# Products of zeros on TensorE after each group of the first and third aggregation of a graph network

## The chip, the core and the metric

The kernel runs on one core of one Trainium2 chip. The metric is the time of one execution in microseconds (us); lower is better. TensorE (PE in the profile) multiplies, VectorE (DVE) and ScalarE (ACT) do elementwise work, GpSimd (POOL) here issues the gathers, SyncE (SP) issues some of the plain DMAs.

## The reference, cut to what matters

Four layers follow each other on 6250 nodes of 256 features; 106,250 directed edges (self loops among them) are sorted by destination. Three times the rows of the source nodes are summed for each destination node.

```python
def _gin_agg(h, src, dst, eps, n_nodes):
    agg = jax.ops.segment_sum(h[src], dst, num_segments=n_nodes)
    return (1.0 + eps) * h + agg

h = _gin_agg(x, src, dst, eps1, n)          # first aggregation, 256 features
h = jax.nn.relu(h @ W1a + b1a)
h = jax.nn.relu(h @ W1b + b1b)
h = _gin_agg(h, src, dst, eps2, n)          # second aggregation, 512 features
h = jax.nn.relu(h @ W2a + b2a)
out = h @ W2b + b2b
...
msgs = h[src] * norm[:, None]               # third aggregation, 256 features
out = jax.ops.segment_sum(msgs, dst, num_segments=N) + b
```

Between the second and third aggregation stands an attention over 64 slices, and behind the third a layer of 8 experts of which each node uses two. Both are untouched by the change.

## The kernel before

**Tiles.** Nodes are split into 49 blocks of 128 (`NB`). The edges of a block are worked off in tiles of 128 edges: POOL gathers the 128 source rows of a tile from a table in HBM into SBUF (line 280, `edge_rows`), DVE makes a matrix of zeros and ones from the edges' destinations (line 295, `onehot`), and TensorE multiplies the two and adds into the PSUM bank of the block, `psA[b % 2]` (line 320; line 330 for those tiles at the end of a block that also hold edges of the next, `early`). The data are fp32, and each such product appears in the trace as two matmul records (passes).

**Groups.** Three tiles make a group (`GT = 3`). Each aggregation has 282 groups and 846 gathers. TensorE waits at the start of a group until its one-hots and gathers are there, and its last product counts up `groups_used`. `edge_rows` is a ring of 8 groups in the first aggregation and of 6 in the other two; POOL waits with the gathers of a group until TensorE has counted the group that had the slot before. DVE waits on the same count for its ring of one-hots.

**What else runs in an aggregation.** Four blocks make a superblock (at the end two of two blocks and one of one: `SUPER`). While the groups of one superblock are summed, the dense work on the one before it is done in 22 steps, put between the groups by `pipeline`. Each engine has its own copy of that order and works it off strictly. `close(b)` takes the sums of a block out of PSUM (DVE, lines 961 and 962, or 1804), transposes them (TensorE, lines 990 or 1907) and copies the transposes (ACT, lines 905 or 1722). The steps of the first aggregation are three dense products on TensorE (lines 1005, 1011, 1017) with ACT and DVE behind each (913, 917, 923, 971). Those of the third are a product (1920), a normalisation and the choice of experts on DVE, transposes (1929, copied by ACT at 1733), gates (1935) and placements (1947, from DVE's tiles of line 1886). The bank `psA` has 512 fp32 columns. The first aggregation uses 257 of them, the second all, the third 256. `zeros` is a constant tile of 128x512 bf16.

Of the kernel before, what the change touches and what calls it, by code (L numbers as in the profile page):

```python
# [35 lines left out]
P = 128  # L36
N = 6250
E = 106250
D = 256
HID = 512  # L40
# [31 lines left out]
SUPER = tuple((b, 4) for b in range(0, 44, 4)) + ((44, 2), (46, 2), (48, 1))  # L72
# [15 lines left out]
def groups_of(b):  # L88

    return groups_before(b + 1) - groups_before(b)  # L90
# [23 lines left out]
def build(nc, a, out):  # L114

    with ExitStack() as whole:
# [59 lines left out]
        def rsqrt(ch, out, x, tmp):  # L176

            v = nc.vector
            ch.link(v.tensor_scalar(tmp.bitcast(I32), x.bitcast(I32), 1, None, ALU.arith_shift_right))
            ch.link(v.tensor_scalar(out.bitcast(I32), tmp.bitcast(I32), -1.0, float(0x5F3759DF), ALU.mult, ALU.add))  # L180
            for _ in range(3):
                ch.link(v.tensor_tensor(tmp, out, out, ALU.mult))
                ch.link(v.tensor_tensor(tmp, tmp, x, ALU.mult))
                ch.link(v.tensor_scalar(tmp, tmp, -0.5, 1.5, ALU.mult, ALU.add))
                ch.link(v.tensor_tensor(out, out, tmp, ALU.mult))

        def pipeline(group, close, piece, begin=None, close_first=False):

# [647 lines left out]
        with ExitStack() as stack:  # L836
            S = Scope(stack, "s1")
            FIRST, SECOND, THIRD = (0, 1, 2, 3), (5, 7, 9, 11), (14, 16, 18, 20)
            edges = Edges(S, table1, T1_W, ((0, D + 1),), FP32, GPB - 1)
            w1a = S.sb("w1a", [P, KD, HID])  # L840
            w1b = S.sb("w1b", [P, KH, HID])
# [135 lines left out]
            def _(pe):  # L977
                mm = nc.tensor.matmul

                def group(b, g):  # L980
                    edges.sums(pe, b, g, psA, s_evac)
                    if b == 0 and g == edges.spare_at:
                        edges.spare_sums(pe, psM[3])

                def close(b):
                    s, q = place_of(b)
# [603 lines left out]
        with ExitStack() as stack:  # L1590
            S = Scope(stack, "s4")

            PRODUCT, NORM, TURNED, GATES = (0, 1, 2, 3), 4, (7, 8, 9, 10), 11
            CHOICE, RANK, PLACED, USED = 12, 16, (17, 18, 19, 20), (18, 19, 20, 21)
            edges = Edges(S, table3, D, ((0, D),), FP32, 1, slots=6)
            w = S.sb("w", [P, KD, D])
            bias = S.sb("bias", [P, D])
# [294 lines left out]
            def _(pe):  # L1892
# [4 lines left out]
                def group(b, g):  # L1897
                    edges.sums(pe, b, g, psA, s_evac)
                    if b == 0 and g == edges.spare_at:
                        edges.spare_sums(pe, psO[1])  # L1900

                def close(b):
                    s, q = place_of(b)
# [315 lines left out]
```

How the kernel before makes its waits and increments, by code:

```python
            def link(self, ins):  # L167
                self.n += 1
                ins.then_inc(self.sem, 1)
                self.eng.wait_ge(self.sem, self.n)
# [94 lines left out]
            def gather(self, pool):  # L265
                for b in range(NB):
                    for i in range(groups_of(b)):
                        g = groups_before(b) + i
                        if g == self.spare_at + 1:
                            with pool.Fori(0, self.spare_count(pool)) as k:
                                pool.wait_ge(self.s_oidx, k * 32 + 32)
                                pool.sem_inc(self.s_ostart, 1)
                                pool.indirect_dma_start(self.o_rows[:, :], None, self.table,
                                                        bass.IndirectOffsetOnAxis(ap=self.o_idx[:, 0:1], axis=0)).then_inc(self.s_orow, 16)
                        if g >= self.SLOTS:
                            pool.wait_ge(self.s_used, g - self.SLOTS + 1)
                        for t in range(tiles_of(b, i)):
                            at = column(b, i) + t
                            pool.indirect_dma_start(
                                self.rows[:, g % self.SLOTS, t, :], None, self.table,
                                bass.IndirectOffsetOnAxis(ap=src_idx[:, at:at + 1], axis=0)
                            ).then_inc(self.s_group[g % self.SLOTS], 16)
# [377 lines left out]
                def first_edges():  # L661
                    dve.wait_ge(s_brow, 16)
                    ch.link(v.tensor_copy(brow_f[:, :], brow[:, :]))
```

## Time and profile before

| | us |
|---|---|
| timed runs, median of 3 | 4537.28 (4523.38 to 4537.72) |
| profiled execution, span from first to last instruction | 4526.2 |
| first aggregation, from its first gather to its last product | 1244.5 |
| second aggregation | 1293.0 |
| third aggregation | 1251.0 |
| gather instructions on POOL, 2538 in all, busy | 2495.4 |
| TensorE matmuls busy in the whole span | 3407.3 |

The three aggregations are 3789 us of the span and are bounded by the time of their groups. "Busy" for TensorE is the union of records whose ends are modelled. The clock that a row shows is the mean of what TensorE was granted, 1.00 being 2.4 GHz and 0.50 being 1.2 GHz.

### The profile page before, as it was taken

To read this page: it belongs to the slowest core of one execution; us is meant where nothing else is said; L and a number is where in the kernel's file an instruction comes from. 1 tells how busy PE (TensorE), PEld (TensorE's weight loads), DVE (VectorE), ACT (ScalarE), POOL (GpSimd) and SP (SyncE) were. 2 spreads that over 40 slices of the span, in tenths; PEclk is the share of its full clock that TensorE was granted. 3 is DMA by queue.
4 is the path that set the end of the run, shared out by engine and by line. 5 is a ranking of instruction groups with operands and counts; after the bars stand their busy time and mean duration, and the time that the engine had idled before them with its cause. 6 is when DMAs were issued, how large, how long until landed. Compare 5 with 4: busy or idle time off the path is not lost. (4 is left out here: it accounts for less than half of the span.)

```text
span 4526.2 us, 40559 instructions
## 1 busy us (share of the span) xinstructions
PE 3407.3 (75%) x12357; PEld 2256.3 (50%) x12359; DVE 1481.5 (33%) x5707; ACT 497.8 (11%) x1161; POOL 2794.2 (62%) x2815
## 2 busy tenths in 40 slices
PE   3577777878878889899999976566556656658997
PEld 2354444545453444444444455345444444438986
DVE  5112121212121433444333445234343343442221
ACT  4010000000110000000000002000000000003432
POOL 4666666666646666666666502666666666635664
PEclk7788888988889999999999987777777778769998
DMA  6333333433349666666666527334334333327887
GB/s 199 90 112 112 111 110 110 131 111 111 109 128 330 194 198 200 193 190 194 195 201 205 170 104 240 108 114 123 115 117 128 115 114 114 119 80 174 203 210 188
DMA packets 321341, 687.10 MB, mean 152 GB/s; under 512 B 58976, under 2 KB 148300, under 8 KB 320854
## 3 DMA queue, kind: packets, MB, share of 16 engines
q0 software_dynamic: 169712, 474.01, 37.9%
q10 hardware_dynamic: 86448, 110.35, 7.4%
q1 hardware_dynamic: 64970, 100.14, 6.8%
q8 instruction: 105, 1.72, 0.2%
q14 instruction: 106, 0.87, 0.1%
HBM read 592.43 MB, written 99.13 MB: 153 GB/s over the span
## 5 line engine op out<-in xcount | busy, mean ns | idle before, releaser
L280 POOL DMA_INDIRECT s_edge_rows<-table,w_src_idx x2538 | 2495.4, 983 | 1235.3 <-issue 712.6
L320 PE MATMUL s_psA<-s_edge_rows,s_onehot 128*128 128x257 f32 (+2 forms) x4932 | 1695.0, 487 | 212.1 <-DMA s_edge_rows<-table,w_src_idx 92.3
L320 PEld LDWEIGHTS s_psA<-s_edge_rows,s_onehot 128*128 128x128 f32 x4932 | 1012.6, 210 | 758.6 <-issue 635.1
L295 DVE TENSOR_SCALAR s_onehot<-w_iota_row,w_dst_l 128x128 f32<-128x128 bf16 x2466 | 531.6, 296 | 28.5 <-PEq L149 16.4
L2031 POOL DMA_INDIRECT acc_rows<-s_y,s_tnode x105 | 166.3, 1584 | 130.7 <-DVE s_y L2154 98.8
L1011 PE MATMUL s_psM<-s_h1T,s_w1b 128*128 128x512 f32 (+2 forms) x448 | 195.2, 582 | 52.5 <-ACT s_h1T L913 49.0
L330 PE MATMUL s_psA<-s_edge_rows,s_early 128*128 128x257 f32 (+2 forms) x648 | 221.3, 468 | 10.2 <-issue 9.0
L1017 PE MATMUL s_psM<-s_w2a,s_hT 128*128 128x512 f32 x392 | 196.3, 647 | 22.7 <-issue 16.6
L2179 PE MATMUL s_psU<-s_xT,s_w 128*128 128x128 f32 x1680 | 208.2, 278 | 0.2 <-ACT s_xT L2085 0.2
L2179 PEld LDWEIGHTS s_psU<-s_xT,s_w 128*128 128x128 f32 x1680 | 199.3, 195 | 0.6 <-issue 0.6
L2189 PE MATMUL s_psD<-moe_w,s_hT 128*128 x840 | 199.5, 381 | 0.0
L971 DVE SCALAR_TENSOR_TENSOR s_own<-s_psM,s_eps,s_b2a 128x512 f32<-128x512 f32 x49 | 36.8, 750 | 451.2 <-ACT s_trow L923 313.3
L961 DVE TENSOR_TENSOR w_degree<-w_degree,s_psA 128x1 f32<-128x1 f32 x49 | 7.4, 152 | 513.7 <-remote 294.4
L1947 PE MATMUL moe_psI<-s_at_tile,s_at_lane 128*128 128x392 f32 x196 | 106.5, 678 | 85.9 <-DVE s_at_tile L1886 72.1
L330 PEld LDWEIGHTS s_psA<-s_edge_rows,s_early 128*128 128x128 f32 x648 | 129.6, 200 | 79.7 <-issue 65.9
L1907 PE MATMUL s_psT<-w_ident,s_agg 128*128 128x128 f32 x98 | 26.3, 362 | 180.7 <-DVE s_agg L1804 117.6
L2189 PEld LDWEIGHTS s_psD<-moe_w,s_hT 128*128 128x128 f32 x840 | 152.4, 191 | 16.6
L1011 PEld LDWEIGHTS s_psM<-s_h1T,s_w1b 128*128 128x128 f32 x448 | 89.5, 208 | 134.1 <-issue 77.1
L2154 DVE SCALAR_TENSOR_TENSOR s_y<-s_psD,s_part,s_yb 128x256 f32<-128x256 f32 x105 | 50.8, 484 | 270.5 <-PE s_psD L2189 257.3
L2094 ACT ACTIVATE s_hT<-s_psU,moe_b 128x128 f32<-128x128 f32 x420 | 119.9, 367 | 169.2 <-issue 101.2
L1017 PEld LDWEIGHTS s_psM<-s_w2a,s_hT 128*128 128x128 f32 x392 | 80.3, 209 | 111.3 <-issue 101.8
L2038 POOL DMA_INDIRECT s_xs<-xl_rows,s_tnode x105 | 103.9, 989 | 38.7 <-issue 31.1
(364 smaller groups left out, 2802.6 us busy)
## 6 DMA issues: line engine op xcount, KB each, us to landing
s_w<-in_L_ffn_W_dram SPq DMA_DIRECT2D x105, 512.0 KB
s_edge_rows<-table,w_src_idx POOLq DMA_INDIRECT x2538
s_swT<-swt_rows SPq DMA_DIRECT2D x12, 1024.0 KB
table<-s_trow ACTq DMA_DIRECT2D x11, 1024.0 KB
own_rows<-s_own ACTq DMA_DIRECT2D x11, 1024.0 KB
s_self_h<-own_rows ACTq DMA_DIRECT2D x11, 1024.0 KB
swt_rows<-s_swT ACTq DMA_DIRECT2D x11, 1024.0 KB
extra_rows<-w_zeros SPq DMA_DIRECT2D x7, 896.0 KB
```

The costliest lines, as they stand in the source:

```text
L280: pool.indirect_dma_start(self.rows[:, g % self.SLOTS, t, :], None, self.table, bass.IndirectOffsetOnAxis(ap=src_idx[:, at:at + 1], axis=0 ...
L295: last = nc.vector.tensor_scalar(into[:, t, :], iota_row[:, q * P:(q + 1) * P], dst_l[:, at + t:at + t + 1], None, ALU.is_equal)
L320: last = nc.tensor.matmul(banks[b % 2][:, 0:w], self.onehot[:, g % self.AHEAD, t, :], self.rows[:, g % self.SLOTS, t, col:col + w], start= ...
L330: last = nc.tensor.matmul(banks[(b + 1) % 2][:, 0:w], self.early[:, b % 2, i * GT + t - (CAP - max(EARLY)), :], self.rows[:, g % self.SLOT ...
L1011: last = mm(psM[m][:, 0:n], w1b[:, c, m * P:(m + 1) * P], h1T[:, c, 0:n], start=c == 0, stop=c == KH - 1)
L1017: last = mm(psM[j][:, :], hT[:, c, j * P:(j + 1) * P], w2a[:, c, :], start=c == 0, stop=c == KH - 1)
L1947: mm(psI[:, 0:SLOT_TILES], at_lane[:, (2 * b + i) % 4, :], at_tile[:, (2 * b + i) % 4, :], start=False, stop=False, skip_group_check=True) ...
L2031: pool.indirect_dma_start(acc_rows, bass.IndirectOffsetOnAxis(ap=tnode[:, t:t + 1], axis=0), y[:, t % 4, :], None, compute_op=ALU.add).the ...
L2038: pool.indirect_dma_start(xs[:, t % RING, :], None, xl3_rows, bass.IndirectOffsetOnAxis(ap=tnode[:, t:t + 1], axis=0)).then_inc(s_xs[t % R ...
L2094: last = ac.activation(hT[:, t % 2, m, :], psU[t % 2][:, m * P:(m + 1) * P], ACT.Relu, bias=b1[:, bass.ds(e, 1), m])
L2179: last = mm(psU[t % 2][:, m * P:(m + 1) * P], w1[:, t % WRING, k, m * P:(m + 1) * P], xT[:, t % 2, k, :], start=k == 0, stop=k == KD - 1)
L2189: last = mm(psD[t % 2][:, 0:D], hT[:, t % 2, k, :], w2[:, bass.ds(e, 1), k, :], start=k == 0, stop=k == KH - 1)
```

## The change

After the products of each group but the last of its block, TensorE also multiplies `zeros` by `zeros`, in bf16, and adds the result into columns of the block's own bank that nobody reads. In the first aggregation these are 8 products of 224 columns (288 to 511), for blocks 0 to 43; in the third, 16 products of 256 columns (256 to 511), for all blocks. They stand behind the instruction that counts up `groups_used`, wait for nothing and count up nothing. In all 209 groups of the first aggregation (1672 products) and 233 of the third (3728 products) have them. Nothing is removed.

```diff
--- before.py
+++ after.py
@@ -183,6 +183,11 @@
                 ch.link(v.tensor_tensor(tmp, tmp, x, ALU.mult))
                 ch.link(v.tensor_scalar(tmp, tmp, -0.5, 1.5, ALU.mult, ALU.add))
                 ch.link(v.tensor_tensor(out, out, tmp, ALU.mult))
+
+        def idle_products(nc, unread, count):
+
+            for _ in range(count):
+                nc.tensor.matmul(unread, zeros[:, 0:P], zeros[:, 0:unread.shape[1]], start=False, stop=False, skip_group_check=True)
 
         def pipeline(group, close, piece, begin=None, close_first=False):
 
@@ -836,6 +841,7 @@
         with ExitStack() as stack:
             S = Scope(stack, "s1")
             FIRST, SECOND, THIRD = (0, 1, 2, 3), (5, 7, 9, 11), (14, 16, 18, 20)
+            IDLE = 8
             edges = Edges(S, table1, T1_W, ((0, D + 1),), FP32, GPB - 1)
             w1a = S.sb("w1a", [P, KD, HID])
             w1b = S.sb("w1b", [P, KH, HID])
@@ -981,6 +987,8 @@
                     edges.sums(pe, b, g, psA, s_evac)
                     if b == 0 and g == edges.spare_at:
                         edges.spare_sums(pe, psM[3])
+                    if b < SUPER[-3][0] and g < groups_of(b) - 1:
+                        idle_products(nc, psA[b % 2][:, D + 32:HID], IDLE)
 
                 def close(b):
                     s, q = place_of(b)
@@ -1592,6 +1600,7 @@
 
             PRODUCT, NORM, TURNED, GATES = (0, 1, 2, 3), 4, (7, 8, 9, 10), 11
             CHOICE, RANK, PLACED, USED = 12, 16, (17, 18, 19, 20), (18, 19, 20, 21)
+            IDLE = 16
             edges = Edges(S, table3, D, ((0, D),), FP32, 1, slots=6)
             w = S.sb("w", [P, KD, D])
             bias = S.sb("bias", [P, D])
@@ -1898,6 +1907,8 @@
                     edges.sums(pe, b, g, psA, s_evac)
                     if b == 0 and g == edges.spare_at:
                         edges.spare_sums(pe, psO[1])
+                    if g < groups_of(b) - 1:
+                        idle_products(nc, psA[b % 2][:, D:HID], IDLE)
 
                 def close(b):
                     s, q = place_of(b)
```

On TensorE, in the first aggregation at the third dense product of blocks 12 to 15, these instructions stand in a row before (in the code after, lines are 5 to 8 higher; 1017 becomes 1025, 990 becomes 998, 320 becomes 325):

```order
L1017 MATMUL s_psM<-s_w2a,s_hT 128x512 x4
L320 MATMUL s_psA<-s_edge_rows,s_onehot 128x257 x6
L990 MATMUL s_psT<-w_ident,s_agg 128x128 x2
L1017 MATMUL s_psM<-s_w2a,s_hT 128x512 x4
L320 MATMUL s_psA<-s_edge_rows,s_onehot 128x257 x6
```

and after the change:

```order
L1025 MATMUL s_psM<-s_w2a,s_hT 128x512 x4
L325 MATMUL s_psA<-s_edge_rows,s_onehot 128x257 x3
L190 MATMUL s_psA<-w_zeros 128x224 x8
L325 MATMUL s_psA<-s_edge_rows,s_onehot 128x257 x3
L190 MATMUL s_psA<-w_zeros 128x224 x8
L998 MATMUL s_psT<-w_ident,s_agg 128x128 x2
L1025 MATMUL s_psM<-s_w2a,s_hT 128x512 x4
L325 MATMUL s_psA<-s_edge_rows,s_onehot 128x257 x3
L190 MATMUL s_psA<-w_zeros 128x224 x8
```

Each group of three is followed by eight products of zeros, so the transposes of line 990 stand 16 products further back.

On TensorE, in the third aggregation at the start of the dense work of a superblock (transposes of the last block's sums, then the products of line 1920), before:

```order
L320 MATMUL s_psA<-s_edge_rows,s_onehot 128x256 x6
L1907 MATMUL s_psT<-w_ident,s_agg 128x128 x2
L320 MATMUL s_psA<-s_edge_rows,s_onehot 128x256 x3
L1920 MATMUL s_psO<-s_w,s_aggT 128x256 x4
L320 MATMUL s_psA<-s_edge_rows,s_onehot 128x256 x3
L1920 MATMUL s_psO<-s_w,s_aggT 128x256 x2
```

and after (1907 becomes 1918, 1920 becomes 1931):

```order
L190 MATMUL s_psA<-w_zeros 128x256 x16
L1918 MATMUL s_psT<-w_ident,s_agg 128x128 x2
L325 MATMUL s_psA<-s_edge_rows,s_onehot 128x256 x3
L190 MATMUL s_psA<-w_zeros 128x256 x16
L1931 MATMUL s_psO<-s_w,s_aggT 128x256 x4
L325 MATMUL s_psA<-s_edge_rows,s_onehot 128x256 x3
L190 MATMUL s_psA<-w_zeros 128x256 x16
L1931 MATMUL s_psO<-s_w,s_aggT 128x256 x2
```

Sixteen products of zeros now stand between every group and the dense product behind it.

## Rows read from the trace of the kernel before

**Rows 1.** First line of the page.
```profile
span 4526.2 us, 40559 instructions
```

**Rows 2.** Busy time in the three aggregations: stretch, length, busy by engine (instructions), clock, DMA.
```profile
71.50:1316.00 1244.50, 936.52 (x2966) 591.34 (x2966) 243.51 (x1078) 126.64 (x213) 816.12 (x847) 0.86 0.39 112
1333.00:2626.00 1293.00, 1155.03 (x3278) 599.08 (x3278) 509.92 (x1573) 97.44 (x155) 858.47 (x848) 0.95 0.68 204
2783.00:4034.00 1251.00, 749.26 (x2674) 566.60 (x2674) 482.07 (x2149) 38.79 (x109) 823.78 (x847) 0.76 0.41 120
```

**Rows 3.** The gathers in the first aggregation and what ended POOL's idle time before them.
```profile
L280 POOL DMA_INDIRECT s_edge_rows<-table,w_src_idx x737: 951/957/1072, 179.3 to 1239.5; - x185
...
  remote: 106.7, 37
  PE s_psA L320: 31.9, 20
  PE s_psA L330: 3.9, 3
```

**Rows 4.** The gathers in the second aggregation and what ended POOL's idle time before them.
```profile
L280 POOL DMA_INDIRECT s_edge_rows<-table,w_src_idx x833: 951/957/2895, 1349.9 to 2599.2; - x167
...
  DMA s_edge_rows<-table,w_src_idx: 92.2, 32
  PE s_psA L320: 65.6, 44
  PE s_psA L330: 16.6, 6
```

**Rows 5.** The gathers in the third aggregation and what ended POOL's idle time before them.
```profile
L280 POOL DMA_INDIRECT s_edge_rows<-table,w_src_idx x801: 951/957/1993, 2800.1 to 3959.3; - x161
...
  DMA s_spare_dst<-dst_pad: 121.1, 49
  PE s_psA L320: 23.5, 20
  PE s_psA L330: 11.1, 4
```

**Rows 6.** TensorE by line, first aggregation: busy us, mean ns | idle before, releasers.
```profile
L1011 PE MATMUL s_psM<-s_h1T,s_w1b 128*128 128x512 f32 x352 | 173.6, 636 | 44.0 <-ACT s_h1T L913 40.5 <-issue 3.2
...
L990 PE MATMUL s_psT<-w_ident,s_agg 128*128 128x128 f32 x84 | 20.5, 333 | 100.2 <-DVE s_agg L962 71.2 <-issue 29.0
```

**Rows 7.** Timeline of the first aggregation: start, us, engine, line [idle before <-releaser].
```profile
562.00 3.59 PE L1017 MATMUL s_psM<-s_w2a,s_hT 128*128 128x512 f32 x8
...
565.44 2.77 PE L320 MATMUL s_psA<-s_edge_rows,s_onehot 128*128 128x257 f32 x12
...
579.07 0.60 ACT L923 ACTIVATE s_trow<-s_psM 128x512 f32<-128x512 f32 x1 [20.12 <-DMA x_xl<-in_x_dram]
...
580.90 0.69 PE L990 MATMUL s_psT<-w_ident,s_agg 128*128 128x128 f32 x2 [12.70 <-DVE s_agg L962]
```

**Rows 8.** Two short windows.
```profile
572.00:576.00 4.00, 0.00 (x0) 0.00 (x0) 0.00 (x0) 0.00 (x0) 2.86 (x3) 0.50 0.37 99
2778.00:2786.00 8.00, 0.00 (x0) 0.10 (x1) 3.55 (x18) 0.00 (x0) 3.20 (x6) 0.50 0.56 158
```

**Rows 9.** TensorE by line, third aggregation.
```profile
L1947 PE MATMUL moe_psI<-s_at_tile,s_at_lane 128*128 128x392 f32 x176 | 95.1, 673 | 71.7 <-DVE s_at_tile L1886 57.9 <-DMA x_xl<-in_x_dram 8.3 <-issue 5.4
...
L1907 PE MATMUL s_psT<-w_ident,s_agg 128*128 128x128 f32 x90 | 24.6, 367 | 180.7 <-DVE s_agg L1804 117.6 <-issue 63.1
L1929 PE MATMUL s_psT<-w_ident,s_xl 128*128 128x128 f32 x88 | 22.0, 341 | 64.2 <-ACT s_xl3T L1733 40.9 <-issue 23.2
```

**Rows 10.** Timeline of the third aggregation.
```profile
3099.50 0.38 PE L1907 MATMUL s_psT<-w_ident,s_agg 128*128 128x128 f32 x2
...
3111.19 0.38 ACT L1722 ACTIVATE s_aggT<-s_psT 128x256 f32<-128x256 f32 x1 [25.50 <-DMA s_swT<-swt_rows]
```

**Rows 11.** The one load of zeros as weights that the trace of before has.
```profile
L1895 PEld LDWEIGHTS moe_psI<-w_zeros x1: 105/105/105, 2782.2 to 2782.2; 128*128 128x128 bf16 x1
```

## Prediction

> **What bounds the kernel now.** I first took the span, 4526.2 us [rows 1]; the median of the timed runs, 4537.28, lies 11.1 above it, and I make the sum in the span's time and add it to the median. Then the windows of the three aggregations [rows 2]. They hold 1244.5 + 1293.0 + 1251.0 = 3788.5 us, 84% of the span. The reader is to see that their lengths hardly differ though TensorE is busy for 936.5, 1155.0 and 749.3 us of them, that is 75%, 89% and 60%. So TensorE's amount of work is not what sets the pace. What the three share is 846 gathers each. A gather takes 957 ns at the median [rows 3 to 5], and the three stretches spend 816, 858 and 824 us in them [rows 2].
>
> Next, what POOL waits for [rows 3 to 5]. Some 0.3 us between one gather and the next are plain issue. Beyond that POOL waits at the start of a group for `groups_used`, which only TensorE counts up. The profile puts part of that wait down to TensorE's products (lines 320 and 330), and part to "remote" or to a DMA that has nothing to do with it; in that part the products were finished by the trace long before. By gather:
>
> first: 106.7/737 = 0.145 us not explained, 35.8/737 = 0.049 explained, 0.193 together;
> second: 92.2/833 = 0.111 and 82.2/833 = 0.099, together 0.209;
> third: 121.1/801 = 0.151 and 34.6/801 = 0.043, together 0.194.
>
> The timeline shows what the unexplained part looks like [rows 7]. Line 1017 has its records from 562.00 to 565.6 and the next two groups follow until 568.2. ACT's copy of that product starts at 579.07, 13.5 us after the end of the records, and TensorE stands until 580.90 for DVE, which was queued behind that copy. In the third aggregation transposes end at 3099.9 and the copy of them starts at 3111.19 [rows 10]. ACT was idle in both cases. The other engines learn of TensorE's work late, by 10 us and more, and the trace doesn't say why. In such a gap the granted clock falls: from 572 to 576 it is 0.50, 1.2 GHz, with TensorE idle [rows 8]. Over an aggregation it is 0.86, 0.95 and 0.76 [rows 2], lowest where TensorE does least.
>
> **The change part by part.** Nothing is removed; 1672 products of 224 columns and 3728 of 256 are added. The trace has no full record of a bf16 product. Its cost from both sides: eight passes of 512 columns in fp32 start 565.44 - 562.00 = 3.44 us apart [rows 7], 0.43 us each or two cycles of 2.4 GHz per column. A bf16 product may go at the same two cycles: 0.187 and 0.213 us. Or at one: the only load of bf16 weights takes 105 ns for 128 columns [rows 11] while the clock is 0.50 [rows 8], 126 cycles of 1.2 GHz. I take one cycle per column, since that row has the same tile of zeros and the same type: 0.093 and 0.107 us at the full clock, twice that at half. The load of the weights lies under the product before it, as the fp32 passes at exactly two cycles per column show. Sum at the full clock: 1672 x 0.093 = 155 us in the first aggregation, 3728 x 0.107 = 399 us in the third. With two cycles it would be 313 and 794 us.
>
> The Trainium skill ("TensorE: Matmul & The Clock Gate", Back-to-back issue gap) gives N / 2.4 + 2.5 ns between bf16 products at the full clock. By that formula they would be 96 and 109 ns, 161 and 406 us together; no run here shows it yet.
>
> How much of this lies beside other work: by the busy times of today's clock, 936.5 + 155 = 1092 of 1244.5 us and 749.3 + 399 = 1148 of 1251.0, 88% and 92% [rows 2]. At the second aggregation's clock the old parts would be nearer 936.5 x 0.86/0.95 = 848 and 749.3 x 0.76/0.95 = 599, an upper bound of what a warmer clock gives, and the shares 81% and 80%. The second aggregation lives with 89%. So in both the products fit into time in which TensorE now waits, and the cover is POOL's gathers. What stands behind a product of zeros in TensorE's queue is the next group or the next dense step. Each may start up to 8 x 0.093 = 0.75 us or 16 x 0.107 = 1.7 us later, and with it the counts for which POOL, ACT and DVE wait. The rings of eight and six groups absorb such a delay as long as TensorE catches up.
>
> The price or gain is then read in POOL's wait per gather. If a denser TensorE brings the unexplained part to the second aggregation's 0.111, that returns (0.145 - 0.111) x 846 = 29 us and (0.151 - 0.111) x 846 = 34 us. Against it the explained part rises. From 0.049 at a share of 75% to 0.099 at 89%, a straight line gives 0.070 at 80 to 81%: +0.021 x 846 = 18 us in the first and +0.027 x 846 = 23 us in the third. Net: -63 + 41 = -22 us, and the forecast 4537 - 22 = 4515 us. Ends of this case: no return of clock and the full 0.099 in both (+89 - 63 = +26), and no rise at all (-63).
>
> **The rivals.**
>
> *A. TensorE keeps its waits and becomes the bound of the third aggregation (slower).* In the window of the third, TensorE waits 57.9 + 117.6 + 40.9 = 216 us for ACT and DVE at the placements and the two transposes [rows 9]. If those waits stay as long as they are and the products come on top, the stretch takes 1148 + 216 = 1364 us instead of 1251: +113, total 4650. The first aggregation has 40.5 + 71.2 = 112 us of such waits [rows 6] and would need 1092 + 112 = 1204, below its 1244.5. It decides from where more than 103 of today's 216 us remain behind the products. For it: gaps like that of 12.7 us [rows 7] are far longer than the 0.75 or 1.7 us of zeros ahead of them, and behind a gap each group of the third now costs 1.7 us more to catch up. Against it: the second aggregation has few such gaps at 89%. At two cycles per column this rival would add some 500 us, which I give almost nothing.
>
> *B. A warm clock removes the late counts (much faster).* If the late counts come from a TensorE that stands and cools, products behind each group would bring them on time. All of POOL's waits are 0.193 x 846 + 0.194 x 846 = 327 us; half of it gone gives 4537 - 164 = 4373. For it: the lower the clock, the larger the unexplained part per gather (0.111 at 0.95, 0.145 at 0.86, 0.151 at 0.76). Against it: total waits per gather are the same 0.19 to 0.21 in all three, so what a dense TensorE saved in one part it lost in the other. The Trainium skill (same page, Loop structure matters more than you think) says that a TensorE that waits between bursts does the next burst at the lower clock; the trace agrees with the 0.50 in the gap, and on that rule the change should help. It says nothing of counts that come late.
>
> *C. Nothing happens.* POOL's gathers and their issue set the pace, the long gaps stay long, and the zeros run in time that nobody needs: 4537. For it: the equal totals of 0.19 to 0.21. The change would then not do what products into unread columns can only be for, to hold the clock.
>
> **How the numbers follow.** Forecast 0.43 (4515, its own range 4474 to 4563), A 0.27 (4550 to 4650), B 0.16 (4373 to 4470), C 0.14 (4523 to 4551). A measurement of this kernel can tell about 0.3%, 14 us. Faster by more than that: 0.30 of the forecast and all of B, 0.46. Within it: 0.09 of the forecast, 0.13 of C, 0.22. Slower: 0.04, A, and 0.01 of C, 0.32. The range of 4400 to 4640 leaves out the far half of B and the end of A, less than 2 in 10.
>
> **What would show it.** Right: mean clock of the first and third aggregation at 0.9 or above; records of line 190 spaced by 0.09 to 0.11 us; POOL's unexplained wait near 0.11 us per gather; TensorE's gaps over 4 us fewer, not only shorter; the second aggregation unchanged. A shows as POOL's wait put down to line 325 rising above 0.1 us per gather in the third aggregation, which grows alone. B shows as ACT's copies starting within a microsecond of the product they wait for. C shows as a clock that stays at 0.86 and 0.76. The prediction is wrong if a product costs two cycles per column, if the counts come late for a reason that more TensorE instructions make worse, or if catching up behind a gap with 16 products in every group empties POOL's ring.

## The result, and the profile after

The changed kernel takes 4599.24 us (median of 4 runs, 4589.41 to 4612.92) beside 4531.9 us for the kernel before: a ratio of 1.0156, 95% interval 1.0136 to 1.0176. It is slower by 1.56% (the two medians lie 67 us apart). A later run of the same kernel gave 1.0169 (1.0146 to 1.0193), and the kernel before against itself 0.9992 (0.9976 to 1.0008). The forecast was 4515 us with a small gain; the time lies in the range given, on the wrong side of no change.

First the head of the page. The span has grown by 78.3 us against [rows 1]; the row PEclk gives the granted clock of TensorE in 40 slices of the span.

```profile
span 4604.5 us, 51359 instructions
...
PE 3892.9 (85%) x17757; PEld 2691.5 (58%) x17759; DVE 1477.1 (32%) x5707; ACT 498.0 (11%) x1161; POOL 2796.1 (61%) x2815
...
PEclk6799989999999999999999987899998989879998
```

Then the same windows of the three aggregations as in [rows 2]: stretch, length, busy us and instructions of PE, PEld, DVE, ACT and POOL, clock, DMA.

```profile
72.00:1341.00 1269.00, 1085.70 (x4638) 726.33 (x4638) 244.80 (x1080) 127.08 (x213) 815.27 (x847) 0.91 0.39 110
1358.60:2647.20 1288.60, 1150.83 (x3278) 596.26 (x3278) 506.70 (x1570) 97.12 (x155) 860.71 (x847) 0.95 0.68 204
2804.40:4111.60 1307.20, 1089.69 (x6402) 871.06 (x6402) 478.43 (x2149) 38.85 (x109) 823.17 (x847) 0.90 0.39 115
```

The reader is to see three things. The clock went where the change sends it: from 0.86 to 0.91 and from 0.76 to 0.90, while the second aggregation stays at 0.95. The second aggregation is as long as it was (1288.6 after 1293.0). And the first is 24.5 us longer, the third 56.2 us. The rest of the kernel adds some 2 us, so the loss lies in the two stages that have the products. In the third TensorE's busy time grew by 1089.7 - 749.3 = 340.4 us and the rest of its time shrank from 501.7 to 217.5 us, by 284.2: it gave back most of what the products took, and the difference is the 56.2 us.

Next come the gathers, with what ended POOL's idle time before them, in the first aggregation and in the third; these answer to [rows 3] and [rows 5].

```profile
L285 POOL DMA_INDIRECT s_edge_rows<-table,w_src_idx x735: 951/957/1081, 180.2 to 1259.8; - x184
...
  remote: 112.8, 48
  PE s_psA L325: 47.9, 26
  PE s_psA L335: 11.2, 5
```

```profile
L285 POOL DMA_INDIRECT s_edge_rows<-table,w_src_idx x810: 951/957/1820, 2819.7 to 4039.1; - x162
...
  DMA s_spare_dst<-dst_pad: 133.2, 71
  PE s_psA L325: 62.0, 44
  PE s_psA L335: 26.3, 16
```

The values by gather, in the prediction's terms: the unexplained wait was 0.145 us in the first aggregation and is 112.8/735 = 0.153; it was 0.151 in the third and is 133.2/810 = 0.164. It should have fallen to 0.111. The explained wait rose from 0.049 to 59.1/735 = 0.080 and from 0.043 to 88.3/810 = 0.109.

The products themselves cost what they were priced at. This is the timeline of the third aggregation: start, us, engine, line.

```profile
3197.00 1.91 PE L190 MATMUL s_psA<-w_zeros 128*128 128x256 bf16 x16
3198.75 0.38 PE L1918 MATMUL s_psT<-w_ident,s_agg 128*128 128x128 f32 x2
```

Sixteen products of 256 columns take 3198.75 - 3197.00 = 1.75 us, 0.109 us each; those of 224 columns start 0.096 us apart, by the median. By the formula of the Trainium skill ("TensorE: Matmul & The Clock Gate", Back-to-back issue gap) it is 109 and 96 ns, and the trace agrees. The sum in the two stages is 1672 x 0.096 + 3728 x 0.109 = 567 us at the full clock.

What TensorE waits for has changed its nature. By line in the third aggregation (busy us, mean ns | idle us before it, releasers), beside [rows 9]:

```profile
L190 PE MATMUL s_psA<-w_zeros 128*128 128x256 bf16 x3728 | 489.4, 282 | 73.2 <-issue 61.9 <-DVE s_spare_own L1796 10.4
...
L1958 PE MATMUL moe_psI<-s_at_tile,s_at_lane 128*128 128x392 f32 x185 | 83.4, 582 | 12.6 <-DVE s_at_tile L1895 11.5 <-issue 1.1
...
L1918 PE MATMUL s_psT<-w_ident,s_agg 128*128 128x128 f32 x96 | 23.4, 326 | 51.1 <-issue 37.0 <-DVE s_agg L1813 14.1
```

The waits for DVE before the placements went from 57.9 to 11.5 us and before the transposes from 117.6 to 14.1. In their place stand 61.9 us before products of zeros that are put down to "issue": TensorE stands and waits for nothing that the profile shows. These products have nothing to wait for, and all 3728 are in the records, so no missing record makes the gap. What is left is that TensorE does not have its next instruction yet; that is an inference, since the trace shows no such event.

### The profile page after: what moved, and what is told of

Its sections match the earlier page's. It is cut to its first block and busy times, and to the rows that moved or that the text cites. A ratio compares the mean times of both kernels' runs of the same rounds, so it can differ in the third digit from the quotient of the medians.

```text
span 4604.5 us, 51359 instructions
## 1 busy us (share of the span) xinstructions
PE 3892.9 (85%) x17757; PEld 2691.5 (58%) x17759; DVE 1477.1 (32%) x5707; ACT 498.0 (11%) x1161; POOL 2796.1 (61%) x2815
## 5 line engine op out<-in xcount | busy, mean ns | idle before, releaser
L325 PE MATMUL s_psA<-s_edge_rows,s_onehot 128*128 128x257 f32 (+2 forms) x4932 | 1644.8, 471 | 129.3 <-issue 74.1
L325 PEld LDWEIGHTS s_psA<-s_edge_rows,s_onehot 128*128 128x128 f32 x4932 | 954.3, 200 | 638.6 <-issue 545.2
L190 PE MATMUL s_psA<-w_zeros 128*128 128x256 bf16 (+1 forms) x5400 | 698.6, 277 | 97.9 <-issue 86.3
L190 PEld LDWEIGHTS s_psA<-w_zeros 128*128 128x128 bf16 x5400 | 540.0, 101 | 249.3 <-issue 138.7
L1019 PE MATMUL s_psM<-s_h1T,s_w1b 128*128 128x512 f32 (+2 forms) x448 | 182.1, 548 | 12.0 <-ACT s_h1T L919 8.6
L1025 PE MATMUL s_psM<-s_w2a,s_hT 128*128 128x512 f32 x392 | 185.3, 618 | 1.0 <-ACT s_hT L923 1.0
L1013 PE MATMUL s_psM<-s_aggT,s_w1a 128*128 128x512 f32 (+2 forms) x224 | 111.7, 644 | 65.0 <-issue 52.7
L1731 ACT ACTIVATE s_aggT<-s_psT 128x256 f32<-128x256 f32 x49 | 18.8, 383 | 1043.6 <-DMA s_swT<-swt_rows 483.5
L1019 PEld LDWEIGHTS s_psM<-s_h1T,s_w1b 128*128 128x128 f32 x448 | 79.9, 192 | 81.8 <-issue 70.5
```

Of the source, the lines that this page charges most:

```text
L190: nc.tensor.matmul(unread, zeros[:, 0:P], zeros[:, 0:unread.shape[1]], start=False, stop=False, skip_group_check=True)
L325: last = nc.tensor.matmul(banks[b % 2][:, 0:w], self.onehot[:, g % self.AHEAD, t, :], self.rows[:, g % self.SLOTS, t, col:col + w], start= ...
L1013: last = mm(psM[m][:, 0:n], w1a[:, c, m * P:(m + 1) * P], aggT[:, c, 0:n], start=c == 0, stop=c == KD - 1)
L1019: last = mm(psM[m][:, 0:n], w1b[:, c, m * P:(m + 1) * P], h1T[:, c, 0:n], start=c == 0, stop=c == KH - 1)
L1025: last = mm(psM[j][:, :], hT[:, c, j * P:(j + 1) * P], w2a[:, c, :], start=c == 0, stop=c == KH - 1)
```

## Experiments

All ratios are against the kernel before on the same chip in the same hour. Stage lengths are from the first gather of a stage to the end of its last product of gathered rows in the trace: 1244.5, 1292.3 and 1251.2 us before, 1268.8, 1288.6 and 1307.2 in the change.

My first theory was rival A in a new form: time of TensorE is what counts, and 567 us of products are more than its waits give back. Its rival: not the time of the products but their number.

**Products in the third aggregation only.**

```diff
-            IDLE = 8
+            IDLE = 0
```

> No products of zeros in the first aggregation, 16 of 256 columns per group in the third as in the change. The third aggregation grew by 56 us and the first by 24 us in the profiles. Time theory (TensorE's own time per group came too near to POOL's 3.8 us per group, so it cannot catch up behind a gap and POOL's ring stays full): the two stages are independent, so this gives about 56/80 of the loss, ratio 1.010 to 1.014, with the first aggregation back at 1245 us. Instruction theory (the number of instructions in TensorE's queue costs): two thirds of the products are here, ratio also near 1.010. If the loss came from the two together or from elsewhere (instruction fetches over the whole run), the first aggregation would stay long.

Measured: 1.0096 (1.0076 to 1.0115). The third aggregation takes 1303.5 us, the first 1248.9. **The first only** (the third's 16 set to 0):

> 8 products per group in the first aggregation, none in the third. If the two places add up: 1.0156 less 1.0096 of the third alone, 1.006 (1.004 to 1.008), with the first aggregation 24 us longer than before and the third unchanged. Rival, that the first's loss is noise of its start: 1.001 or less.

Measured: 1.0042 (1.0026 to 1.0057), the first aggregation 1261.2 us and the third 1248.1. The two places add up to 1.0138, within the interval of the change. The first aggregation's loss is real though small.

**A quarter, half, and fewer products that take longer.** In order: 2 and 4 products in place of 8 and 16; the same 2 and 4 with fp32 zeros; 4 and 8.

> A quarter of the products: 2 per group in the first aggregation, 4 in the third. They take 0.19 and 0.44 us per group at the full clock instead of 0.76 and 1.74. Time theory: TensorE keeps its room to catch up, POOL's explained wait stays near that of before (0.05 us per gather) and the ratio is 0.993 to 1.002; with a clock that rises a little. Instruction theory: a quarter of the loss, ratio near 1.004. If the loss is linear in the added time, also 1.004.

```diff
-                nc.tensor.matmul(unread, zeros[:, 0:P], zeros[:, 0:unread.shape[1]], ...)
+                nc.tensor.matmul(unread, zeros[:, :].bitcast(FP32)[:, 0:P], zeros[:, :].bitcast(FP32)[:, 0:unread.shape[1]], ...)
```

> A quarter of the products, but of zeros read as fp32, which take four cycles per column instead of one (two passes of two cycles): the same added time per group as the change (0.75 and 1.7 us), with half of its matmul and weight-load records. Time theory: the same loss as the change, ratio 1.012 to 1.019. Instruction theory: half of the loss or less, ratio 1.002 to 1.008.

> 4 products per group in the first aggregation and 8 in the third, half of the change. If only the number of instructions counts, this stands where 2 and 4 fp32 products stood, which are two instructions pairs each: 1.008 (1.006 to 1.010), although its columns take half as long. If the column time counts, it lies below that: 1.003 to 1.006. Straight line between none and the change: 1.008; between a quarter (1.0009) and the whole: 1.006.

**Sixteen as before, but of 8 columns.**

```diff
-                nc.tensor.matmul(unread, zeros[:, 0:P], zeros[:, 0:unread.shape[1]], ...)
+                nc.tensor.matmul(unread[:, 0:8], zeros[:, 0:P], zeros[:, 0:8], ...)
```

> As many products as in the change (8 and 16 per group) but of 8 columns: nearly no column time, yet the same number of products and loads of weights. A product then costs what its load of weights costs, some 0.05 us at the full clock by the rows of line 190 (128 columns at one cycle), so 0.4 and 0.9 us per group, half of the change. Time theory: a third of the loss or less, ratio 0.998 to 1.006. Instruction theory: all of the loss, ratio 1.012 to 1.019.

Measured, with the number of multiplications recorded for the zeros and their array time by the median spacing in each trace. An fp32 product is recorded as two passes and is also two in the stream of instructions: the instruction queue moves 126 packets in the fp32 kernel with its 1350 calls, as many as in the half with its 2700.

| kernel | multiplications | array time, us | ratio (95%) | clock |
|---|---|---|---|---|
| quarter | 1350 | 142 | 1.0009 (0.9995 to 1.0022) | 0.882 |
| half | 2700 | 283 | 1.0066 (1.0046 to 1.0086) | 0.895 |
| fp32, a quarter of the calls | 2700 | 561 | 1.0080 (1.0058 to 1.0103) | 0.925 |
| 8 columns | 5400 | 135 | 1.0135 (1.0111 to 1.0159) | 0.878 |
| the change | 5400 | 567 | 1.0156 (1.0136 to 1.0176) | 0.916 |

The table decides between the two theories. Rows with the same number lie close together, with intervals that overlap, though their array time differs by a factor of two or four; rows with nearly the same array time (142 and 135, 561 and 567) lie far apart. The products of 8 columns start 0.025 us apart, so in the third aggregation they add about 93 us of array time where the change adds 406, and the stage still takes 1289.9 us in place of 1307.2: 38.7 of the 56 us are there without the columns. (The Trainium skill, TensorE: Matmul & The Clock Gate, Wait — 56ns, not 53.3ns?, says that starts of products never come closer than about 25 ns however small they are; the trace agrees.) What counts is mostly how many instructions TensorE is given. The loss isn't linear from zero: the first 1350 cost next to nothing, the next 1350 26 us, as ratios times 4535.

What the short ones do can be seen in a timeline of that kernel, with TensorE's rows only:

```profile
3311.60 0.69 PE L325 MATMUL s_psA<-s_edge_rows,s_onehot 128*128 128x256 f32 x2 [0.26 <-issue]
3312.14 0.19 PE L190 MATMUL s_psA<-w_zeros 128*128 128x8 bf16 x2
3313.03 0.26 PE L190 MATMUL s_psA<-w_zeros 128*128 128x8 bf16 x4 [0.70 <-issue]
3314.45 0.17 PE L190 MATMUL s_psA<-w_zeros 128*128 128x8 bf16 x1 [1.16 <-issue]
3315.17 0.18 PE L190 MATMUL s_psA<-w_zeros 128*128 128x8 bf16 x1 [0.56 <-issue]
3316.58 0.17 PE L190 MATMUL s_psA<-w_zeros 128*128 128x8 bf16 x1 [1.23 <-issue]
3317.32 0.33 PE L190 MATMUL s_psA<-w_zeros 128*128 128x8 bf16 x7 [0.57 <-issue]
```

From 3312.14 on the zeros, which wait for nothing, come in ones, twos and fours, at 0.7 us or twice 0.7 us from each other; then seven at once. In the third aggregation of this kernel about 100 products start 0.66 to 0.76 us after the product before on the same line; in the change there are about 35, in the kernel before about a dozen. Over the stretch from 2820 to 4040 TensorE's idle time put down to "issue" is 19% of the 8-column kernel and 10.5% of the change. Before, it was 14.6% from 2800 to 3960, but half of that at the transposes (lines 1907 and 1929).

**The same number of instructions without the array.**

```diff
-            for _ in range(count):
-                nc.tensor.matmul(unread, zeros[:, 0:P], zeros[:, 0:unread.shape[1]], ...)
+            for i in range(2 * count):
+                nc.tensor.sem_inc(W.idle[i % 4], 1)
...
+        W.idle = [W.sem(f"idle{j}") for j in range(4)]
```

> Each product of zeros is replaced by two increments of a count that nobody reads, given by TensorE's queue: as many instructions as a product's weight load and multiplication (10,800 in all), but none for the array. Theory 'the number of TensorE instructions, whatever they do': as the short products, 1.013 (1.010 to 1.016). Theory 'the array: each small load and multiplication costs TensorE or what it reads': nothing is left, 1.000 (0.998 to 1.002). Both theories expect the granted clock of before, 0.86. If the stretches in which TensorE's instructions come one by one at steps of about 0.7 us come from the supply of instructions, they grow here too.

Measured: 1.073 (1.0697 to 1.0764), far outside both. The timeline of the third aggregation says why:

```profile
3295.82 1.03 PE L326 MATMUL s_psA<-s_edge_rows,s_onehot 128*128 128x256 f32 x4
3300.99 0.66 PE L1919 MATMUL s_psT<-w_ident,s_agg 128*128 128x128 f32 x2 [4.15 <-issue]
...
3304.06 2.41 PE L326 MATMUL s_psA<-s_edge_rows,s_onehot 128*128 128x256 f32 x6
3309.93 2.30 PE L1959 MATMUL moe_psI<-s_at_tile,s_at_lane 128*128 128x392 f32 x3 [3.46 <-issue]
```

Behind a group come 32 increments, and TensorE's next row is 4.15 us after the end of the last: up to 0.13 us per increment on TensorE's queue, more than a whole product. The third aggregation takes 1553.7 us. So this run doesn't hold the cost of an instruction equal, and can't decide what I made it for. It shows one thing in passing. In the first aggregation, with 16 increments per group and no product added, the stage takes 1266.9 us, as with the change's products (1268.8). So a loss of that size needs nothing in the array. It doesn't follow that the change's loss has the same cause, since 16 increments at up to 0.13 us hold TensorE's queue longer than 8 products at 0.096 us do.

**Is the ring too short?** If TensorE frees slots late now and then, deeper rings should help. Two slots more in the third aggregation, with the change and without it:

```diff
-            edges = Edges(S, table3, D, ((0, D),), FP32, 1, slots=6)
+            edges = Edges(S, table3, D, ((0, D),), FP32, 1, slots=8)
```

> The change, with eight instead of six slots of three tiles in the third aggregation's ring of gathered rows. If the loss there is that TensorE frees slots too late for the gathers, two slots more (8 us of gathers) take most of it away: third aggregation 30 us or more shorter than in the change, ratio 1.003 to 1.009. If the gathers are slowed otherwise (the DMA queues' own limit, or what they share), the third stays 55 us longer and the ratio 1.013 to 1.017.

> The kernel before, with eight instead of six slots in the third aggregation's ring. Theory 'before, the gathers wait there for slots whose release comes late now and then, while TensorE has time to catch up': two slots more take half of the third's 145 us of waits away, ratio 0.985 (0.980 to 0.992). Theory 'TensorE sets the pace there too': as in the change with eight slots, nothing, 1.000.

Measured: 1.0168 (1.0148 to 1.0187) and 1.0018 (1.0008 to 1.0027), the third aggregation 1306.8 and 1258.9 us. My theory of bursts fell, twice. The kernel before, with eight slots:

```profile
L280 POOL DMA_INDIRECT s_edge_rows<-table,w_src_idx x801: 951/957/1997, 2799.2 to 3959.7; - x161
...
  DMA s_spare_dst<-dst_pad: 117.1, 44
  PE s_psA L320: 24.7, 16
  PE s_psA L330: 16.4, 5
```

The unexplained wait is 117.1 us where [rows 5] have 121.1. What changed is only how far the gathers run ahead. From the end of a group's last gather to the start of its products, by the median of the stage's 282 groups, passed 10.7 us before and 18.3 with eight slots (18.5 and 27.2 with the zeros). The ring fills up, however long it is. That is what is seen when the consumer sets the pace. In both kernels, then, TensorE's side (its work, the late counts, its waits for what others do with its results) sets the pace of the third aggregation, and its idle time wasn't spare. Which of these three it is, this test doesn't say.

**Less work for TensorE.** The one-pass products cut the rows to bf16, and nothing else is left out:

```diff
+            def half(self, x):
+                return x.bitcast(BF16).rearrange("p (c two) -> p c two", two=2)[:, :, 1] ...
...
-                        last = nc.tensor.matmul(..., self.onehot[:, g % self.AHEAD, t, :],
-                                                self.rows[:, g % self.SLOTS, t, col:col + w], ...
+                        last = nc.tensor.matmul(..., self.half(self.onehot[:, g % self.AHEAD, t, :]),
+                                                self.half(self.rows[:, g % self.SLOTS, t, col:col + w]), ...
```

> The change, but in the third aggregation the products of gathered rows read only the upper halves of their fp32 numbers, as bf16 (so the rows are cut short before they are added; nothing else is left out). Each group's products become one pass where fp32 takes two: 930 products fewer in the records, and about 1.07 us less of array time per group, 300 us in the stage. Theory 'with the zeros TensorE sets the third aggregation's pace, with its work and the time in which it has no instruction': the stage falls back to 1,251 us or below, ratio 1.000 to 1.004, although all zeros are still there. Theory 'the zeros slow the gathers in another way (a shared path, late counts)': it stays at 1.013 or above.

> The kernel before with the same shorter products of gathered rows in the third aggregation. Theory 'before, TensorE does not set the pace there': 0.995 to 1.002. Theory 'what TensorE does always sets it, by late releases in proportion to its work': clearly faster, 0.985 or less, and then the next run but one says how much of it comes back in the change.

Measured: 1.0138 (1.0116 to 1.016) with the zeros, 0.9954 (0.9938 to 0.997) without. The third aggregation takes 1274.4 and 1235.0 us. So 300 us of array time at the full clock (930 products, two passes of 0.216 us against one of 0.114) gives 33 and 16 us back. By the records TensorE's busy time in the stage fell by 204 and 282 us, though its clock fell too, to 0.80 and 0.58: without the zeros most of the shorter products start 0.213 us apart, which is the lower clock. TensorE's array time isn't the bound either. The window of the first of the two:

```profile
2820.00:4040.00 1220.00, 855.25 (x5273) 611.95 (x5272) 452.53 (x1979) 37.60 (x103) 803.11 (x825) 0.80 0.40 119
```

TensorE is busy for 855 of 1220 us there, its clock is 0.80, and 283 us of its idle time are "issue": by the waits, 303 times. In the change the same stretch has 139 such times. TensorE does a group faster, and then has no instruction.

**The same zeros in longer rows**, 32 behind every second group:

> The change, with the third aggregation's zeros in every second place, 32 at a time in place of 16 at each: the same number within one in a hundred. If TensorE's total counts (work and missing instructions, averaged over the ring): 1.0156 as the change (1.013 to 1.018). If a long row of short instructions runs TensorE out of them, more idle time without a cause in the trace and over 1.02.

Measured: 1.0184 (1.0155 to 1.0214), the third aggregation 1313.0 us. The interval overlaps that of the change. The idle time under "issue" is somewhat larger (163 us where the change has 128). How the zeros are grouped makes no difference to the time that is clear of the noise.

**More time at the ends of blocks.** With the next theory (the waits for TensorE's own late counts at a block's end set the pace) I moved these ends:

```diff
-                    if g == 1 and b and not close_first:
+                    if g == 3 and b and not close_first:
...
-                        if s and i == 2 + k * (len(turns) - 2) // STEPS:
+                        if s and i == 5 + k * (len(turns) - 5) // STEPS:
```

> The kernel before, with each block's transposes on TensorE and ScalarE two groups later (behind the fourth group of the next block, where they stood behind its second) and all the steps of a super-block three groups later. Theory 'TensorE's waits at a block's end for its own late counts set the pace': of the 180 us of waits before the transposes in the third aggregation and the 100 in the first, half or more go, ratio 0.97 to 0.985. Theory 'the gathers set the pace with late releases that no order on TensorE changes': 1.000 (0.997 to 1.003).

> The same later ends of blocks, with the products of zeros of the change. Under the first theory the zeros have used up those waits already, and this gives little: 1.010 to 1.015. Under the second theory also as the change, 1.013 to 1.017; so this run only says whether the zeros' loss stays when the order has more room.

> The kernel before with both the one-pass products of the gathered rows (cut to bf16) and eight slots in the third aggregation. With less work TensorE waited 173 us for gathered rows there while the gathers still waited 123 us for slots: bursts. Theory 'TensorE stands still for longer than the ring lasts, then catches up': two slots more take half of the gathers' waits away, ratio 0.984 (0.980 to 0.990). Theory 'ring depth never matters, the counts come late whatever the lead': 0.995 as without the slots.

> The kernel before, with only the steps of a super-block two groups later and the blocks' ends where they stood. The wait of the dense products for the copies of the transposes (10.6 us at its longest) goes, the wait for the blocks' sums stays: by the first theory a small gain, 0.993 to 1.000; by the second 1.000.

Measured: 1.0135 (1.0118 to 1.0152), 1.0194 (1.0177 to 1.0211), 1.0003 (0.9994 to 1.0013) and 1.0067 (1.005 to 1.0084). But these four can't be read by the expectations, since the kernel before itself took 4084.66 us in this set (13 runs, 4078.36 to 4092.16), on the chip on which it had taken 4529.23 in the set before. It has no trace in this condition; the four kernels made from it do. The windows of the later ends without zeros, then with them:

```profile
62.50:1144.00 1081.50, 889.43 (x2904) 568.15 (x2905) 242.53 (x1074) 123.17 (x203) 816.07 (x847) 0.93 0.45 129
1184.70:2352.80 1168.10, 1109.91 (x3253) 577.64 (x3254) 498.21 (x1541) 93.57 (x152) 865.18 (x847) 0.98 0.74 225
2532.90:3631.90 1099.00, 722.81 (x2653) 539.47 (x2654) 466.49 (x2087) 37.23 (x106) 832.66 (x847) 0.85 0.46 136
```

```profile
62.90:1143.60 1080.70, 997.44 (x4575) 695.75 (x4576) 243.64 (x1075) 123.08 (x203) 815.68 (x847) 0.98 0.46 129
1183.90:2351.40 1167.50, 1112.58 (x3252) 579.50 (x3253) 498.35 (x1542) 93.50 (x152) 867.05 (x847) 0.98 0.74 225
2531.60:3649.50 1117.90, 1003.48 (x6380) 827.79 (x6381) 468.01 (x2088) 38.05 (x106) 831.90 (x847) 0.98 0.46 134
```

And the gathers of the first aggregation in the kernel with the zeros:

```profile
L285 POOL DMA_INDIRECT s_edge_rows<-table,w_src_idx x846: 952/957/1080, 62.7 to 1135.3; - x170
...
  issue: 249.8, 820
...
  PE s_psA L325: 7.0, 23
  PE s_psA L335: 0.6, 2
```

Here the unexplained waits are gone, from every kernel of the set: no "remote" stands among the releasers, and 7.6 us are left of the 172 us of waits in the change's first aggregation. The gathers alone make up the aggregations, 1081 us for 846 of them. TensorE's "issue" time is nearly gone too, and the starts at a distance of 0.7 us with it (none in the zeros of the second kernel). In this condition the first aggregation holds 1672 products of zeros for nothing: 1081.5 and 1080.7 us. The third is 18.9 us longer, 1117.9 after 1099.0, with TensorE busy for 1003 us of it. The two kernels stand to each other as 1.0194/1.0135 = 1.0058. The later ends themselves cost 57 us there. They can win nothing where the gathers bind, and they put the last steps of each stage off: outside the three aggregations lie 799.5 us of the span with them, and 735 in the kernel whose ends stand where they stood, with lighter products and eight slots. That kernel takes 4084.6 us: less work for TensorE and a deeper ring give nothing here.

So I ran the change and the kernel before once more, unaltered.

> The change, unaltered. Where the kernel before takes 4,085 us in this job: if the loss is made by late counts and missing TensorE instructions, it falls to what two kernels with and without the zeros differed by there (1.0194 against 1.0135), 1.006 (1.002 to 1.009), and the gathers wait for slots as rarely as without the zeros. If the loss is TensorE's added work whatever the condition, 1.0156 again. Where the kernel before takes 4,530 us again: 1.0156 (1.013 to 1.018), a repetition.

> The kernel before, unaltered, for its trace: a ratio of 1.000 (0.998 to 1.002) in either case. Where it takes 4,085 us: gathers that wait for slots once or twice per aggregation, TensorE waiting for gathered rows for a fifth of the time, and no row of instructions at 0.7 us.

Measured: 1.0169 (1.0146 to 1.0193) and 0.9992 (0.9976 to 1.0008); the kernel before took 4529.53 us, so the condition was back and this is a repetition. The stages agree with the first traces: 1271.7, 1288.7 and 1306.9 us for the change, 1247.8, 1287.7 and 1248.2 for the kernel before. The change alone without the late counts wasn't measured; the pair with later ends is the nearest.

**How late the counts come, in every trace.** Two distances can be read in all traces: for each of POOL's waits of over 1 us, from the recorded end of the product that frees the slot to the gather (median); and for the 49 copies of the transposes on ACT (lines 1722 and 905 of the kernel before), how many start over 2 us after the transposes ended and ACT was free. First and third aggregation:

| kernel | POOL's waits over 1 us | from product to gather, us | late copies of 49 |
|---|---|---|---|
| before, two traces | 51, 60; 59, 57 | 11.8, 11.1; 11.5, 11.6 | 17, 18; 16, 21 |
| quarter | 55, 64 | 7.1, 7.6 | 3, 18 |
| half | 66, 81 | 7.8, 6.5 | 20, 31 |
| fp32, a quarter of the calls | 72, 91 | 7.3, 4.9 | 24, 22 |
| 8 columns | 79, 107 | 6.8, 5.0 | 27, 30 |
| increments | 71, 118 | 7.8, 0.3 | 22, 0 |
| the change, two traces | 82, 113; 84, 116 | 4.9, 3.5; 5.0, 3.5 | 25, 20; 28, 23 |
| the four of the 4085 us set | 0, 0 to 4 | none, 0.3 | 0, 0 |

In the set at 4085 us every copy follows its transposes at once:

```profile
2805.89 0.38 PE L1907 MATMUL s_psT<-w_ident,s_agg 128*128 128x128 f32 x2
2806.31 0.38 ACT L1722 ACTIVATE s_aggT<-s_psT 128x256 f32<-128x256 f32 x1 [19.84 <-PE s_psT L1907]
```

So the late counts are in all traces of the other sets and in none of this one. The zeros don't make POOL's counts later: the more TensorE is given, the sooner they come behind their product, and the more waits there are. Why both go together isn't shown. The quarter's first aggregation has almost no late copies and is as long as before (1248.5 us), and with the increments the third has none and is the longest (1553.7): late copies and a long stage can be had one without the other.

No kernel here that computes the whole reference beats the kernel before.

## Why the prediction was wrong

**Right:** the price of a product (0.093 and 0.107 us forecast, 0.096 and 0.109 measured), the clock of both aggregations at 0.9 or above, fewer long gaps (TensorE's gaps over 4 us in the third went from 39 with 364 us to 17 with 107), and an unchanged second aggregation.

**The step that failed first** is "if a denser TensorE brings the unexplained part to the second aggregation's 0.111". It had 63 us of gain in it, and went to 0.153 and 0.164: in the stretches' terms +7 and +11 us. The inference was from three stages in a row, clock against unexplained wait, and the second aggregation differs from the others in more than its clock. With this term at zero the forecast would have been 41 us slower than before.

**The second** is the straight line that gave the explained part +18 and +23 us. It measured (0.080 - 0.049) x 846 = 26 us in the first and (0.109 - 0.043) x 846 = 56 us in the third. It drew the wait over TensorE's busy share, and a share can't tell 16 instructions of 0.11 us from one of 1.7. The second aggregation's 89% is reached with 3278 multiplications, the third's 83% in the change with 6402. By the table above, the number weighs more than the time. The share put into the line was too low as well: 80 to 81% forecast, 1085.7/1269.0 = 86% and 83% measured, since the old work didn't shrink with the clock as much as its upper bound allowed. With the measured shares the same line gives +31 and +30 us. So in the first aggregation the line nearly holds (26), and in the third (56) it fails. The two steps together give +100 us of waits; the stages grew by 24.5 + 56.2 = 81, since a gather behind a wait no longer pays the whole of its 0.3 us of issue: all of POOL's time between gathers, issue included, grew by 26 and 50 us. The split itself was weak. Of POOL's waits over 1 us in the third, 152 of 162 us before and 170 of 225 us in the change passed after the freeing product had ended by the records, so most of the "explained" part is late counts too.

**The reading beneath both** was "so TensorE's amount of work is not what sets the pace", and from it "both products fit into time in which TensorE now waits". The first half holds: 300 us less of array time gave 16 to 33 us. The second doesn't follow. The ring is full however deep it is, so TensorE's side sets the pace of the third, by its waits on late counts and the time in which it has no instruction; how much each has of it wasn't separated.

**Rival A** had the right sign, the right place and the wrong mechanism. The waits for DVE and ACT didn't stay behind the products, they shrank (216 us to 11.5 + 14.1 at the lines shown above and 16.7 at the third, 42 together), and the stage grew by 56 where A had 113. Its sign, over 0.1 us per gather from TensorE's products in the third aggregation, came true only with both lines together (0.109; line 325 alone 62.0/810 = 0.077). The first aggregation, which A left alone, lost 24.5 us too.

**Rival B** is refuted by the clock: in the third it went from 0.76 to 0.90 and the unexplained wait per gather didn't fall. Its condition came true in part, since the counts came sooner (the table above), and it still gained nothing. The rule of the Trainium skill (TensorE: Matmul & The Clock Gate, Loop structure matters more than you think) held as far as it goes, since denser work kept the clock up. It brought nothing, as array time wasn't the bound. Of the signs named at the end of the prediction, "the counts come late for a reason that more TensorE instructions make worse" is nearest, but only in part: the waits became more (60 to 113 in the third), the distance from product to gather shorter (11.1 to 3.5 us).

**What stays open** is why TensorE's counts and instructions come late in all sets but one, on four chips, and why more instructions lengthen a stage under that condition. Not shown is that one is the cause of the other. They were present in the same sets and absent in the same one. The profile's instruction queue moves one packet of 16 KB per 128 multiplications (105 packets before, 148 in the change), yet of the 48 packets in the first and third aggregation of the kernel before only 2 fall into one of TensorE's 79 gaps over 2.5 us, which are a quarter of the time; so the fetches seen there don't explain the gaps. The quarter's near-zero loss, below the line of the others, isn't explained.

## What to carry to other kernels

Before filling an engine's idle time, ask whether it is spare: deepen the ring ahead of it by a step. If the lead grows and the time doesn't, the engine's side sets the pace, though it may stand idle for 40% of the time. Price what is added by its number of instructions as well as by its array time; if the clock must be kept up by idle work, few long products cost less than many short ones (2700 fp32 passes brought the clock to 0.925 for 0.8%, 5400 bf16 products to 0.916 for 1.6%), and none of them paid here. And if all rivals rest on a wait that the trace doesn't explain, don't book a gain from it by likeness to another stage.

## What the runs showed of the hardware

- The same kernel took about 4530 us in five sets of runs (medians 4527 to 4535) and 4085 us in one, 9.8% less, at one level within each set to 0.6%, on a single core. The difference is POOL waiting for TensorE's counts: 51 to 63 waits over 1 us per aggregation (155 to 167 us) against none to seven in the kernels traced in the other set. A trace that shows ACT idle for 11 us behind a finished product [rows 10] is of the first condition; in the other, each of ACT's copies of the transposes starts 0.04 us after them or after ACT's own work.
- Under that condition TensorE at times gets its instructions at steps of about 0.7 us, also where they wait for nothing.
- An increment of a count by TensorE's own queue cost up to 0.13 us, more than a bf16 product of 256 columns (0.109).
- A bf16 product of 8 columns with its weight load starts 0.025 us after the one before; 256 columns in fp32 take two passes of 0.216 us.
